# Second convolution of three batch pairs by position blocks, turned by VectorE in PSUM

## The reference

```python
h = x.transpose(0, 2, 1)
h = conv1d_grouped(h, conv1_w, conv1_b, c)      # 256 -> 1024 channels, 5 taps
h = gelu(h)
h = conv1d_grouped(h, conv2_w, conv2_b, c)      # 1024 -> 256 channels, 5 taps
h = h.transpose(0, 2, 1)
h = layernorm(h + x, ln0_g, ln0_b)
for i in range(4):
    h = linear_attention(h, ...)
```

## Time and profile before

| | us |
|---|---|
| median of 3 runs | 1835.23 |
| all runs | 1830.85, 1835.43, 1835.23 |
| the profiled execution | 1831.92 |
| its span | 1830.1 |
| TensorE busy in it | 1807.1 (99%) |
| VectorE busy | 1454.8 (79%) |
| ScalarE busy | 937.0 (51%) |
| POOL busy | 1016.3 (56%) |
| granted TensorE clock, mean | 0.999 |

### The profile page before, as it was taken

The page is one execution under the profiler, slowest core; times in us unless marked ns, Lnnn a source line. Parts: engine busy times, 40 slices in busy tenths (PEclk is TensorE's granted clock), DMA queues, the critical chain, the costliest instruction groups (busy, mean ns, idle before and its releaser), DMA issues.

```text
span 1830.1 us, 46210 instructions
## 1 busy us (share of the span) xinstructions
PE 1807.1 (99%) x19196; PEld 1477.9 (81%) x19196; DVE 1454.8 (79%) x3454; ACT 937.0 (51%) x1741; POOL 1016.3 (56%) x775
## 2 busy tenths in 40 slices
PE   9999999999999999999999999999999999999998
PEld 3336888888888888888887988888888888888887
DVE  3667788888788888888887767888888888888887
ACT  5554776677667766677667742232323232323231
POOL 1557999999899999999984012222222222222221
PEclk9999999999999999999999999999999999999999
DMA  8372210100102210000105931010101010101000
GB/s 296 149 270 109 94 60 3 37 2 2 37 2 106 94 37 3 30 9 3 60 2 192 306 105 35 28 42 24 47 24 47 24 47 24 46 25 43 27 12 24
DMA packets 25234, 115.38 MB, mean 63 GB/s; under 512 B 4480, under 2 KB 5440, under 8 KB 19904
## 3 DMA queue, kind: packets, MB, share of 16 engines
q1 hardware_dynamic: 21104, 89.69, 13.9%
q0 software_dynamic: 1152, 12.58, 1.9%
q10 hardware_dynamic: 2768, 10.15, 1.5%
HBM read 80.95 MB, written 31.46 MB: 61 GB/s over the span
## 4 chain that ended last, share of the span: by engine, by line
PE 96%; DVE 2%; issue 1%; DMA 1%; ACT 1%; POOL 0%; ACTq 0%; SPq 0%; DVEq 0%; POOLq 0%
PE bankC L1449 13%; PE bankC L33 7%; PE bankC L32 7%; PE bankC L34 7%; PE ring L32 6%; PE ring L34 6%; PE ring L33 6%; PE bankC L1448 6%; PE big L934 5%; PE big L34 3%; PE big L33 3%; PE big L32 3%; PE ring L866 3%; PE big L846 3%; PE conv_ps L256 3%; PE hid_ps L245 3%
## 5 line engine op out<-in xcount | busy, mean ns | idle before, releaser
L1449 PE MATMUL bankC<-down,act_hi 128*128 128x512 f32 x992 | 353.1, 397 | 0.0
L1448 PE MATMUL bankC<-down,act_lo 128*128 128x256 f32 x868 | 246.2, 284 | 0.0
L1449 PEld LDWEIGHTS bankC<-down,act_hi 128*128 128x128 f32 x992 | 186.3, 188 | 41.9
L1574 DVE TENSOR_TENSOR act_lo<-gel,act_hi 128x512 fp32r<-128x512 f32 x256 | 210.6, 823 | 8.7
L33 PE MATMUL bankC<-aT_lo,up_hi 128*128 128x512 f32 x512 | 199.6, 390 | 0.0
L32 PE MATMUL bankC<-aT_hi,up_hi 128*128 128x512 f32 x512 | 199.5, 390 | 0.0
L34 PE MATMUL bankC<-aT_hi,up_lo 128*128 128x512 f32 x512 | 199.4, 389 | 0.0
L1528 POOL TENSOR_TENSOR hC<-hC,vecC 128x1024 f32<-128x1024 f32 x16 | 38.7, 2416 | 283.5 <-PE turn L1423 283.5
L1534 POOL TENSOR_TENSOR rstdC<-var_epsC,minus_halfC 128x4 f32<-128x4 f32 x47 | 56.1, 1193 | 249.2 <-DVE var_epsC L1602 249.2
L1448 PEld LDWEIGHTS bankC<-down,act_lo 128*128 128x128 f32 x868 | 164.1, 189 | 1.4
L774 POOL TENSOR_TENSOR kr<-kr,kc 128x512 f32<-128x512 f32 x128 | 161.8, 1299 | 0.0
(11 more groups left out here) (215 smaller groups left out, 5261.4 us busy)
## 6 DMA issues: line engine op xcount, KB each, us to landing
raw_late<-in_AB SPq DMA_DIRECT2D x30, 320.0 KB, 3.9
u<-hA SPq DMA_DIRECT2D x8, 1024.0 KB, 5.0
u_next<-u SPq DMA_DIRECT2D x8, 1024.0 KB, 5.9
hC<-u SPq DMA_DIRECT2D x16, 512.0 KB, 3.9
xC<-in_x SPq DMA_DIRECT2D x16, 512.0 KB, 4.8
out<-w_flat SPq DMA_DIRECT2D x15, 512.0 KB, 2.6
w_flat<-in_AB SPq DMA_DIRECT2D x22, 320.0 KB, 3.7
w_split<-w_parts ACTq DMA_DIRECT2D x4, 1536.0 KB, 5.8
```

The lines of the kernel that those rows point to most:

```text
L1448: e.matmul(bank[:, 0:H], a_lo[:, fb, tok], both[k][:, 0, fb, :], start=False, stop=False)
L1449: m = e.matmul(bank[:, :], a_hi[:, fb, tok], both[k][:, :, fb, :], start=fb == 0, stop=fb == FB - 1)
L1574: e.tensor_tensor(a_lo[:, fb, :], g, a_hi[:, fb, :].bitcast(F32), ALU.subtract).then_inc(s_act_lo, 1)
```

## The change

For pair 0 all stays. For pairs 1 to 3:

- `conv2(n)` makes 32 products of a 128x32 tile with 128 columns. The 512 columns of a group j are cut in four blocks of positions k, and each goes through its own column tile to its own 32 partitions. Even blocks are written to `conv_ps`, odd ones to `back_ps` (`turn_ps`).
- VectorE turns the bank in place, 32x32 by 32x32 (`turn`), and adds it to rows of x into `y` (`add_rows`); no `add_input`, no `to_tokens`, no `keep_rows`. The rows of `y` are contiguous, 256 channels a token.
- The rows of x come from HBM in position order into `xt`, by halves of 128 channels (`load_rows`: four DMAs a half, 512 pieces of 512 B each), and POOL adds the second bias to them (`add_bias`, four additions of 128x1024 a pair: steps 4 to 7 for pair 1, steps 14, 16, 18, 20 for pair 2, 22, 24, 26, 28 for pair 3). One more DMA brings the bias row.
- `xt` lies over `cos_k` and `sin_k`, so these two tables are loaded later, each when its half of `xt` is no longer read. x of pair 3 is now loaded when conv1 has read the part it overwrites.

```diff
@@ conv_phase
+    C = 32 * CP
+    BIAS_AT = {4: (1, 0, 0), 5: (1, 0, 1), 6: (1, 1, 0), 7: (1, 1, 1)}
+    for q in range(2, PAIRS):
+        for k in range(4):
+            BIAS_AT[CP * q - 2 + 2 * k] = (q, k // 2, k % 2)
...
+        turn_ps = [conv_ps[:, :], flat(back_ps)]
+        xt, row2 = place["xt"], place["bias2_row"]
...
@@ sync
-                    w.wait_ge(s_convT, CP * (q - 2) + FIRST[k + 1])
+                    if q == 2:
+                        w.wait_ge(s_convT, FIRST[k + 1])
+                    elif q > 2:
+                        w.wait_ge(s_hid, ROWS * (CP * (q - 2) + FIRST[k + 1]))
...
+            def load_rows(q, half):
+
+                if q > 1:
+                    w.wait_ge(s_y, CP * (q - 1) + (half + 1) * CP // 2)
+                cols = slice(half * C // 2, (half + 1) * C // 2)
                 for b in range(2):
...
+                    src = rows_x[2 * q + b, :, cols].rearrange("(m p s) c -> m p s c", m=MT, p=P)
+                    for m in range(MT):
+                        e.dma_start(xt[:, half, (MT * b + m) * S:(MT * b + m + 1) * S, :], src[m]).then_inc(d_xt[half], 16)
...
-            prep.sync(e)
+            prep.sync(e, [0])
+            for half in range(2):
+                load_rows(1, half)
+            prep.sync(e, range(1, prep.L))
             for q in range(PAIRS - 1):
                 if q + 2 < PAIRS:
                     load(q + 2)
                 if q == PAIRS - 2:
 
-                    w.wait_ge(s_convT, CP * (PAIRS - 1))
+                    w.wait_ge(s_hid, ROWS * CP * (PAIRS - 1))
                     load_tables_q(e)
-                store(q)
+                for b in range(2):
+                    if q + 2 < PAIRS:
+                        load_rows(q + 2, b)
+                    if q == PAIRS - 2:
+                        w.wait_ge(s_y, CP * (PAIRS - 1) + (b + 1) * CP // 2)
+                        load_tables_k(e, b)
+                    store(q, b)
...
@@ gpsimd
+            def add_bias(q, half, part):
+
+                w.wait_ge(d_eye, 2 * 16)
+                w.wait_ge(d_xt[half], 2 * MT * 16 * q)
+                rows = xt[:, half, part * TILES // 2:(part + 1) * TILES // 2, :]
+                bias = row2[:, half * C // 2:(half + 1) * C // 2].unsqueeze(1).broadcast_to([P, TILES // 2, C // 2])
+                e.tensor_tensor(rows, rows, bias, ALU.add).then_inc(s_xt, 1)
...
+                if n in BIAS_AT:
+                    add_bias(*BIAS_AT[n])
...
@@ tensor
+                if n >= CP:
+                    w.wait_ge(s_convT, CP)
+                    if n > CP:
+                        w.wait_ge(s_y, max(CP, n - 1))
+                    out = turn_ps[r].rearrange("p (j b m g) -> p j b m g", j=ROWS, b=2, m=MT)
+                    for j in range(ROWS):
+                        for d in range(2):
+                            tokens = hidden[:, r, j, :, d:d + G].rearrange("p b (m k g) -> p b m k g", m=MT, k=ROWS)
+                            for k in range(ROWS):
+                                m = e.matmul(out[32 * k:32 * k + 32, j, :, :, :], band2[:, cp, j, d, :], tokens[:, :, :, k, :],
+                                             start=d == 0, stop=d == 1)
+                    m.then_inc(s_conv, 1)
+                    return
...
-                if 0 <= n - LAG < STEPS:
+                if 0 <= n - LAG < CP:
                     to_tokens(n - LAG)
...
@@ vector
+            def turn(n):
+                w.wait_ge(s_conv, n + 1)
+                e.transpose(turn_ps[n % 2], turn_ps[n % 2]).then_inc(s_back, 1)
+
+            def add_rows(n):
+
+                q, cp = n // CP, n % CP
+                half, c = cp * 2 // CP, cp % (CP // 2) * 32
+                w.wait_ge(s_back, n + 1)
+                w.wait_ge(s_xt, 4 * (q - 1) + 2 * half + 2)
+                w.wait_ge(s_ln, TILES * (q - 1))
...
+                e.tensor_tensor(block(out[:, :, cp * 32:cp * 32 + 32]), turned, block(xt[:, half, :, c:c + 32]),
+                                ALU.add).then_inc(s_y, 1)
...
-                if 0 <= n - LAG < STEPS:
+                if 0 <= n - LAG < CP:
                     keep_rows(n - LAG)
...
-                if 0 <= n - 1 < STEPS:
+                if 0 <= n - 1 < CP:
                     add_input(n - 1)
+                elif n - 1 < STEPS and n:
+                    turn(n - 1)
+                    add_rows(n - 1)
```

More of the change, by code:

```diff
@@ L86, in conv_phase @@
         back_ps = pb("back_ps", [P, 2 * MT, P])
+        turn_ps = [conv_ps[:, :], flat(back_ps)]
+        xt, row2 = place["xt"], place["bias2_row"]
+        d_xt, s_xt = [sem(f"d_xt{h}") for h in range(2)], sem("xt")
         d_eye, d_bias1, d_bias2 = sem("d_eye"), sem("d_bias1"), sem("d_bias2")
@@ L316, in scalar @@
                     prep.scalar(e, layer)
-            w.wait_ge(s_convT, STEPS)
+            w.wait_ge(s_conv, STEPS)
             first()
@@ L337, in keep_rows @@
                 e.tensor_copy(y[q % 2][:, :, cp, :], back_ps[:, :, :]).then_inc(s_y, 1)
+            def turn(n):
[7 more added lines that the diff above has]
+                w.wait_ge(s_ln, TILES * (q - 1))
+                block = lambda a: a.rearrange("p t (j c) -> p t j c", j=ROWS)
+                out = y[q % 2][:, :, :, :].rearrange("p g a b -> p (g a b)").rearrange("p (t c) -> p t c", c=C)
+                turned = turn_ps[n % 2].rearrange("p (j t c) -> p t j c", j=ROWS, c=8)
+                e.tensor_tensor(block(out[:, :, cp * 32:cp * 32 + 32]), turned, block(xt[:, half, :, c:c + 32]),
+                                ALU.add).then_inc(s_y, 1)
             e.memset(convT[:, :, 0:P], 0.0).then_inc(s_idle, 1)
@@ L380, in scalar @@
                     t = S * g + s
-                    e.activation(h[:, t, :].rearrange("p (a c) -> p a c", c=8), token_tile(PAIRS - 1, g, s), ACT.Identity,
-                                 bias=offset[:, t:t + 1], scale=rstd[:, t:t + 1]).then_inc(s_ln_last, 1)
+                    e.activation(normal_tile(PAIRS - 1, t), token_tile(PAIRS - 1, g, s), ACT.Identity, bias=offset[:, t:t + 1], scale=rstd[:, t:t + 1]).then_inc(s_ln_last, 1)
             @staticmethod
@@ L387, in sync @@
                 store_batch(e, PAIRS - 1, b)
-        free = {"hidden": [(s_conv, STEPS)], "ring": [(prep.s_v, 2), (prep.s_v, 2), (s_convT, STEPS), (s_y, STEPS)],
+        free = {"hidden": [(s_conv, STEPS)], "ring": [(prep.s_v, 2), (prep.s_v, 2), (s_y, STEPS - 1), (s_y, STEPS)],
                 "biases": [(prep.s_v, 3)]}
@@ L518, in due, with sync @@
         return [l for l in range(self.L) if n == (2 + 6 * l if l else 3) + after]
-    def sync(self, e):
-        for l in range(self.L):
+    def sync(self, e, layers):
+        for l in layers:
             e.dma_start(self.raw[:, l, :, :].rearrange("p c n -> p (c n)"), self.wqkv[l:l + 1].rearrange(
@@ L1895, in build @@
         under(ctx, [("w_first", weights, F32R)], [("w_flat", [P, 4 * 3 * H])])
-        under(ctx, [("rot", [P, P]), ("kv_mask", [P, CB, 32]), ("mean_mask", [P, CB, 32])], [("zero", [P, 512], F32R)])
-        under(ctx, [("raw_late", [P, 3, width])], [("act1_hi", [P, 8, 512], F32R)], [("cos_k", rows), ("sin_k", rows)])
+        under(ctx, [("rot", [P, P]), ("kv_mask", [P, CB, 32]), ("mean_mask", [P, CB, 32]), ("bias2_row", [P, H])], [("zero", [P, 512], F32R)])
+        under(ctx, [("raw_late", [P, 3, width])], [("act1_hi", [P, 8, 512], F32R)],
+              [("xt", [P, 2, 2 * TILES, H // 2])], [("cos_k", rows), ("sin_k", rows)])
         under(ctx, [("band1", [P, CP, 2, 4, 32]), ("band2", [P, CP, 4, 2, 32]), ("xs1", [P, CP, T // 2 + 1])], [])
@@ L1928, in load_tables @@
         def load_tables(e):
-            e.dma_start(flat(place["cos_k"]), t["cos_k"]).then_inc(keep["d_k"], 16)
-            e.dma_start(flat(place["sin_k"]), t["sin_k"]).then_inc(keep["d_k"], 16)
             e.dma_start(flat(place["gain"]), t["gain_rows"].partition_broadcast(P)).then_inc(keep["d_rows"], 16)
@@ L1936, in load_tables, with load_tables_k @@
             e.dma_start(flat(place["mean_mask"]), t["mean_mask"]).then_inc(keep["d_masks"], 16)
+        def load_tables_k(e, part):
+            name = ("cos_k", "sin_k")[part]
+            e.dma_start(flat(place[name]), t[name]).then_inc(keep["d_k"], 16)
         def load_tables_q(e):
```

32 lines of the change are left out of this document (20 added, 12 removed).

## The result

The changed kernel takes 1844.07 us (median of 6 runs, 1841.75 to 1846.49), the kernel before in runs beside it 1833.32 us (1830.85 to 1835.43): a ratio of 1.0059 [1.0048, 1.0070]. The forecast was 1825.0 us with a range of 1817 to 1840. Direction and range are both missed: the change costs 10.8 us where the forecast's sum had 8.7 to be gained.

What follows compares the result with a forecast made beforehand. TensorE was taken to bound the kernel (96% of the chain). Terms -12.4 - 0.9 - 0.9 + 5.5 = -8.7 us gave 1823.2 from the profiled execution, 1826.5 from the median; forecast 1825.0 us, range 1817 to 1840.

Steps and rivals of the forecast that it cites:

- Part 2: Second convolution on TensorE: 8 products of 512 columns become 32 of 128, 64 records taking 1.85 us.
- Turns: Convolution steps 10 to 30 on TensorE: the turns leave the chain, 21 x 0.59 = 12.4 us less.
- The 32 products: Second convolution of a block: 64 records of 128 columns take 1.85 us, bounds 1.70 to 2.46.
- Rival D: Second convolution: weight loads are exposed, 3.6 us for 1.85, about 1857 us in all; chance 0.05.
- The change of pair: TensorE's waits where the pair changes go: 0.44 us twice, 0.9 us less.
- The end: From the end of conv1(31) to the first attention work: 4.88 us instead of 5.83, 0.9 us less.
- POOL late at steps 14 and 20: Bias addition behind weight preparation delays POOL's edges; TensorE idles 2.7 us twice, 5.5 us given back.
- Rows of x: Loads of x rows for later halves: estimated 6 to 7 us, room 8.8 us, no cost.
- rival C: Rows of x land late at POOL's bias addition, holding up TensorE: +6.0 us, 1841; chance 0.13.
- VectorE: Turn in PSUM (0.72 us) and addition (0.69 us) replace 0.75 + 0.69 us per block: fits, no cost.

Runs made afterwards that it cites:

- e1: The kernel before with 16 small products (64 instructions) added behind the convolutions; 1841.64 us, ratio 1.0042.
- e2: The changed kernel with 48 small products (192 instructions) added behind the convolutions; 1838.22 us, ratio 1.0025 to the kernel before.
- e7: The kernel before with 32 small products added behind the convolutions; 1833.04 us, ratio 1.0000.
- e8: The kernel before with 48 small products added behind the convolutions; 1840.04 us, ratio 1.0040.
- e12: The changed kernel with 16 small products added behind the convolutions; 1835.54 us, ratio 1.0011 to the kernel before.
- e9: The kernel of e6 with 16 small products behind the convolutions instead of 48; 1830.69 us, ratio 0.9983 to the kernel before.
- e10: The kernel of e6 with 16 small products right at the start instead of 48 behind the convolutions; 1828.33 us, ratio 0.9976 to the kernel before.
- e5: The changed kernel without POOL's bias additions and with rows of x loaded for pair 1 only; 1839.44 us (one run).
- e11: The kernel of e6 with eight small products at the start and eight behind the convolutions, instead of 48 there; 1830.60 us, ratio 0.9983 to the kernel before.
- e6: The changed kernel with bias additions on VectorE, POOL's second-layer weight load behind its last convolution step, 48 small products behind the convolutions; 1833.12 us, ratio 0.9998 to the kernel before.

## Why the prediction was wrong

**The step that failed: the sum priced the 32 products by TensorE's busy time alone.** Part 2 weighed what the 64 records stream, issue and load, and had no term for the supply of the instructions, neither there nor for the code behind. That term is the miss. In the convolutions it is 7.3 us: the four products with a stop took 4.02 (from 96.46), 3.15 (104.29), 3.87 (115.05) and 3.85 us (140.67) instead of 1.90 or 1.91. Behind them it is the moved borders, shown by e1, e2, e7, e8 and e12: 9.0 us in the attention, 6.6 to the end, since the kernel before loses 2.4 us to a slower clock and smaller differences behind 981 us. Together 13.9 us of the 18.7 that lie between the forecast of -8.7 and the +10.0 measured.

The terms one by one, in the profiled executions:

- *Turns, -12.4*: right. They are gone from 21 steps, and nothing took their place in the steps without a stop.
- *The 32 products, 1.85 us*: 1.90, so +1.0 us over 21 blocks. The bounds of 1.70 to 2.46 held it. Rival D is out: L308 shows 64 loads of 0.11 us, 7 us in sum, inside 1.90 us. By the rule of the Trainium skill that I weighed (TensorE: Matmul & The Clock Gate, Part 3) loads of the same row group would not overlap; the trace disagrees.
- *The change of pair, -0.9*: right, three steps of 3.80 from 83.14 to 94.56.
- *The end, -0.9*: right. From the end of conv1(31) at 148.45 to the start of conv2(31) pass 2.89 us (3.03 said), in all 4.87 to 153.32 where the earlier trace rows had 5.83.
- *POOL late at steps 14 and 20, 2 x 2.7*: the place was right, the size not. Behind step 14 it cost 4.5 us, 3.2 idle and 1.35 of half clock. The second is covered: POOL's addition ended at 106.17 and the edges 0.42 us later, and TensorE, which the stops of 97.92 and 105.32 had held up by 2.1 and 1.25 us, came to that product only at 107.44; without them it would have stood there for 2.5 us. So 4.5 against 5.5, and the 7.3 us of stops hold 2.5 that would have been lost anyway.
- *Rows of x, nothing*: rival C happened once in three. At the first half of pair 3 they came 11.7 us after their issue began, just beyond the 8.8 us of room, and cost 2.3 us. I had read the empty queue of the earlier trace rows, and had neither priced SP's issuing (4.96 us for the four) nor seen POOL's load of 1.5 MB at the same moment.
- *VectorE, nothing*: its forms cost what was said (0.73 and 0.69 us). What I missed is that POOL's additions and VectorE's preparation of weights slow each other: 1.1 us in step 4. With 0.6 us in the first 16 us, conv1(9) begins 1.7 us late, at 47.40 instead of 45.72. The cause of the 0.6 is open: the granted clock was 0.83 from 10 to 20 us (1.00 before), but with 1.00 there e9 and e10 are as late. The step that the kernel before begins at 15.32 begins at 15.91 in the changed one, at 15.95 in e9 and at 15.90 in e10.

These come to 1.0 - 1.0 + 2.3 + 1.7 = 4.0 us; with 13.9 that is 17.9 of 18.7, and 0.8 us stay unexplained.

Could it have been seen? The kernel before had ten rows of "issue" in its attention, 6.6 us in products that wait for nothing, each with a packet of the instruction queue some 2.4 us ahead of its end. Had I counted the change's instructions, a rival "the attention's borders move" would have stood beside C and raised the chance of a loss; its size, though, no row of the kernel before could have told.

## What to carry to other kernels

Count the instructions that a change adds to the bounding engine, not only their time: where the chain shows "issue" inside dense runs of small products, moving the code by 64 instructions was worth 7 to 8 us of 1830 either way in the medians (e1, e12, and e8 against e7). A change of under 1% is judged with a few padding instructions beside it as well: in a better position this one costs 0.11% instead of 0.59%, and with POOL's additions on VectorE and the late load it gains 0.17 to 0.24%. And where old waits of the bounding engine are taken away, stops of this kind can appear in their place.

## What the runs showed of the hardware that I had not expected

- A block of 256 of TensorE's instructions is one packet of 16 KB, and all 213 stops of the fourteen traces stand at the same place of such a block; 2.2 to 3.0 us pass from the start of the packet to the first product behind a stop, in the convolutions and in the attention alike, in one case 3.9 (e9).
- 64 instructions more ahead of the attention cost 8 us, 128 nothing, 192 6.7 us (e1, e7, e8).
- After an idle time of 3.2 us (changed kernel, 76.7 to 79.9) or of 3.55 us (e9, 128.36) the granted clock was 0.50 over the next products, and so it was after 1.99 us (e5, 127.23) and 2.18 us (e2, 97.28); after 1.91 and 1.56 us (changed kernel, 97.92 and 116.50) and 2.28 us (e11, 92.80) it was 1.00.
- VectorE adds the same 128x1024 rows in 1.22 us that take POOL 2.35, and with it there L631's form is back at 1.01 us on average (e6, e10), where beside POOL's addition one took 3.13.
